# Neighbour sums of a graph layer: key one-hots made for four units in one 16-bit comparison

## What is computed

```python
agg = jax.ops.segment_sum(x[src], dst, num_segments=x.shape[0])
h = x + agg
```

## Time and profile before

| | us |
|---|---|
| median of 3 runs | 3819.62 |
| lowest and highest | 3816.06, 3821.36 |
| the profiled execution | 3812.78 |
| its span | 3811.0 |
| busy in the span: PE, DVE, POOL, ACT | 3136.0, 2677.0, 2500.8, 1944.4 |
| first and last start of the row one-hots (L1933) | 3367.4, 3688.0 |
| first and last start of the sums (L1945) | 3379.6, 3693.1 |

### The profile page before, as it was taken

How to read it: one execution, slowest core, us unless ns; L and a number is a source line. 1 busy time by engine, 2 the same in 40 slices (tenths; PEclk the granted TensorE clock), 3 DMA queues, 4 the chain that set the end, 5 groups by cost and what they waited for, 6 DMA issues and landing times. The chain is left out here.

```text
span 3811.0 us, 89063 instructions
## 1 busy us (share of the span) xinstructions
PE 3136.0 (82%) x31400; PEld 1856.8 (49%) x31400; DVE 2677.0 (70%) x6673; ACT 1944.4 (51%) x5497; POOL 2500.8 (66%) x1949
## 2 busy tenths in 40 slices
PE   0369999999999999994629799797997978559886
PEld 0235555555555555553515455453554535347663
DVE  3538888888888888886745466464664647489972
ACT  3346556666665666651306455454554544158761
POOL 4488787687687687406378888888888870557620
PEclk9989999999999999996759899898998988579997
DMA  3323333333333333214222233232332322211210
GB/s 62 59 51 75 79 82 82 76 88 83 75 84 80 75 90 82 70 53 100 57 46 63 58 74 75 61 75 60 70 75 61 75 60 44 40 32 38 44 41 22
DMA packets 417512, 249.11 MB, mean 65 GB/s; under 512 B 258173, under 2 KB 380449, under 8 KB 416562
## 3 DMA queue, kind: packets, MB, share of 16 engines
q0 software_dynamic: 97392, 70.80, 10.8%
q10 hardware_dynamic: 237600, 89.88, 9.3%
q1 hardware_dynamic: 82086, 82.74, 8.7%
HBM read 135.21 MB, written 105.95 MB: 63 GB/s over the span
## 5 line engine op out<-in xcount | busy, mean ns | idle before, releaser
L1011 PE MATMUL L_e_ps_z<-L_e_xT,L_w_abs 128*128 128x500 f32 x2700 | 1382.6, 622 | 193.1 <-ACT L_e_rl L1127 192.3
L598 POOL DMA_INDIRECT L_e_tiles<-in_x_dram,src_tile x800 | 1107.9, 1385 | 350.3 <-issue 234.1
L598 POOL DMA_INDIRECT L_e_tiles<-x_d,src_tile x800 | 1010.2, 1263 | 250.2 <-issue 237.7
L1127 ACT ACTIVATE L_e_rl<-L_e_ps_z 128x500 f32<-128x500 f32 x1350 | 778.8, 586 | 573.0 <-PE L_e_ps_z L1011 571.0
L1319 DVE SCALAR_TENSOR_TENSOR L_e_acc<-L_e_acc,L_e_row,L_e_ps_v 128x130 f32<-128x130 f32 (+1 forms) x1440 | 447.4, 311 | 620.2 <-PE L_e_ps_v L1073 434.4
L1011 PEld LDWEIGHTS L_e_ps_z<-L_e_xT,L_w_abs 128*128 128x128 f32 x2700 | 444.7, 191 | 480.1 <-issue 370.1
L642 ACT ACTIVATE L_e_xs<-L_e_tiles 125x64 f32 x1800 | 308.8, 248 | 390.1 <-issue 255.6
L1073 PEld LDWEIGHTS L_e_ps_v<-L_e_xs,L_e_p 125*64 125x64 f32 x8400 | 318.3, 141 | 357.8 <-issue 175.8
L1073 PE MATMUL L_e_ps_v<-L_e_xs,L_e_p 125*64 125x65 f32 x8400 | 425.8, 235 | 19.4 <-DVE L_e_acc L1319 15.5
L1118 ACT ACTIVATE L_e_xT<-L_e_ps_x 128x500 f32<-128x500 f32 x450 | 264.8, 588 | 236.5 <-PE L_e_ps_x L998 236.4
L1230 DVE SCALAR_TENSOR_TENSOR L_e_f<-L_e_rl,L_sign,L_e_f 128x500 f32<-128x500 f32 x450 | 329.1, 731 | 9.9 <-ACT L_e_rl L1127 6.6
(11 more groups left out here) (323 smaller groups left out, 4211.0 us busy)
## 6 DMA issues: line engine op xcount, KB each, us to landing
L_v_d<-L_e_acc ACTq DMA_DIRECT2D x225, 260.0 KB
L_e_dlb<-dloc_d SPq DMA_DIRECT2D x90, 468.8 KB, 5.1
L_v_d<-L_e_acc ACTq DMA_DIRECT2D x225, 130.0 KB
L_e_tiles<-in_x_dram,src_tile POOLq DMA_INDIRECT x800
L_e_tiles<-x_d,src_tile POOLq DMA_INDIRECT x800
L_e_lim<-limits_d SPq DMA_DIRECT2D x180, 39.1 KB
L_max_d<-L_e_me SPq DMA_DIRECT2D x45, 78.1 KB
L_e_lim<-limits_d SPq DMA_DIRECT2D x180, 19.5 KB
```

The costliest lines, as they stand in the source:

```text
L598: pool.indirect_dma_start(lay.tiles[:, g % TR * D:(g % TR + 1) * D], None, lay.x_rows, bass.IndirectOffsetOnAxis(k.src_tile[:, g:g + 1], 0 ...
L1011: pe.matmul(ps_z[part % ZR][:, 0:QT], lay.w_abs[:, part * 128:(part + 1) * 128], xT[q][:], start=True, stop=True).then_inc(s["z_ready"], 1)
L1127: act.activation(rl[n % NE][:], ps_z[part % ZR][:, 0:QT], ACT.Relu, scale=1.0 - SLOPE).then_inc(s["relu_done"], 1)
```

## The change

The key one-hots are made as the row one-hots are: one comparison for four units, units innermost, with both operands bf16 tensors. For this a table `keys4` holds each of the 200 keys four times, and `key16` holds `key_of` in bf16; both are made once, by two DVE instructions at the head of the block ahead of the turns. A ring of 3 buffers of four units takes the place of 10 buffers of one. A count matmul now reads its streamed operand with a step of four elements (8 bytes), where it read adjacent elements. The semaphore `hot` rises by four with each comparison.

```diff
-    HR, KR, CR, PQ = 3, 10, 3, 4
+    HR, KR, CR, PQ = 3, 3, 3, 4
...
+        keys4 = sbuf(nc, octx, nm + "keys4", [T, KEYS, HU], BF16)
+        key16 = sbuf(nc, octx, nm + "key16", [T, EU], BF16)
...
                 def _(dve):
+                    dve.tensor_copy(keys4[:], keys_n[:].unsqueeze(2).to_broadcast([T, KEYS, HU]))
+                    dve.tensor_copy(key16[:], key_of[:])
                     dve.wait_ge(s["part"], 1)
...
-            ohk = [sbuf(nc, ctx, f"{nm}ohk{r}", [T, KEYS], BF16) for r in range(KR)]
+            ohk = [sbuf(nc, ctx, f"{nm}ohk{r}", [T, KEYS, HU], BF16) for r in range(KR)]
...
-                            pe.matmul(ps_c[n % 2][0:RW, u * KEYS:(u + 1) * KEYS], ohr[v // HU % HR][:, :, v % HU], ohk[v % KR][:],
+                            pe.matmul(ps_c[n % 2][0:RW, u * KEYS:(u + 1) * KEYS], ohr[v // HU % HR][:, :, v % HU], ohk[v // HU % KR][:, :, v % HU],
                                       start=True, stop=True).then_inc(s["counted"], 1)
...
-                    def hot_keys(v):
-                        if v >= KR:
-                            dve.wait_ge(s["counted"], v - KR + 1)
-                        dve.tensor_scalar(ohk[v % KR][:], keys_n[:], key_of[:, v:v + 1], None, ALU.is_equal).then_inc(s["hot"], 1)
+                    def hot_keys(g):
+                        if g >= KR:
+                            dve.wait_ge(s["counted"], (g - KR + 1) * HU)
+                        dve.tensor_tensor(ohk[g % KR][:], keys4[:],
+                                          key16[:, g * HU:(g + 1) * HU].unsqueeze(1).to_broadcast([T, KEYS, HU]),
+                                          ALU.is_equal).then_inc(s["hot"], HU)
...
                             if u % HU == 0:
                                 hot_rows((i * GR_U + u) // HU)
-                            hot_keys(i * GR_U + u)
+                                hot_keys((i * GR_U + u) // HU)
```

## The result

| | before | changed |
|---|---|---|
| median of the runs, us | 3820.49 | 3874.05 |
| lowest and highest | 3816.06, 3822.50 | 3872.22, 3877.01 |
| the profiled execution | 3812.78 | 3873.93 |
| its span | 3811.0 | 3872.1 |
| stage, first row one-hot to the end of the last sum | 326.0 | 378.8 |

The change is slower: ratio 1.0145, 95% interval 1.0129 to 1.0161, 54 us by the medians. The forecast was 3793, range 3784 to 3811.

A forecast was written before the change was run, and what follows sets the result against it. DVE was taken as the bound. Turns 281, block waits 11, start 2 and ends 4 gave a 298 us stage against 326; -28 + 0.5 + 0.3 = -27 from the median 3819.6 gave 3793, range 3784 to 3811.

The forecast's parts named there:

- the unpriced piece: Count matmuls on PE reading 200 columns 8 bytes apart: addition between 0 and 85 ns a matmul, taken as 0.
- the strided stream at double rate: Rival on PE's 1024 count matmuls: 0.085 us more each, three quarters showing, 65 us; +38, so 3858; chance 0.10.
- The cost on DVE: Key comparison of 800 elements takes 0.49 us, not held up beside gathers; a DVE turn becomes 3.70 us.
- What is late next: PE and ACT set the pace: turns of 4.15 us, 4.70 with `add_block`; stage 298 us against 326.
- The added pieces: Two DVE instructions ahead of the turns, 0.5 us; PE's first wait for four units, 0.3; ring of 12 units, nothing.
- The rival of the f32 rate: DVE's key comparison takes 0.91 us, turns 5.38 us, DVE stays the bound: +19, so 3838; chance 0.02.

The follow-up runs named there:

- the adjacent stream: The changed kernel, but each count matmul streams 200 adjacent elements of the four-unit one-hot, so counts are of the wrong keys: 3799.49 us, ratio 0.9946.
- the pairs: The changed kernel with each unit's 200 keys adjacent, each key number stored twice in a row and no `keys4`: 3801.71 us, ratio 0.9951.
- the run with units outermost: The changed kernel with each unit's 200 keys adjacent, the comparison reading each key number 200 times in a row, no `keys4`: 3886.33 us, ratio 1.0157.

## Why the prediction was wrong, point by point

**The step that failed** is the unpriced piece: "I take 0". Between an addition of 0 and of 85 ns a count matmul, the value is the upper end, 0.085 us. The reason given for 0 was that the weight loads' 15 ns says nothing of the stream; true, but it left no row that says 0 either. Advanced Engine Details and Errata, section SBUF Cachelines, of the Trainium skill, by which two reads on each 16-byte line are at full speed, is contradicted for this stream: at 8 bytes two reads fall on a line, and a count matmul takes 0.17 us instead of 0.085.

**The rival that came true** is the strided stream at double rate, given 0.10. Its mechanism and place were right, its price was low: 1024 x 0.085 = 87 us, of which I let three quarters show, because PE has slack behind j = 0 and 1. But only one pair's slack is left there. In a turn without `add_block` seven of the eight steps from pair to pair grow by 0.17 to 0.19 us and one stays, 1.27 us in all; in the 19 turns with both `add_block` and `add_rows` all eight grow, 1.44 us. With each of 63 turns at the shortest of its kind, the sum is 276.7 us with the adjacent stream and 359.6 with the change, so 83 of the 87 us show.

Some of it is made up in the seven turns with the first use of a block. They lie 18.8 us above their pace with the adjacent stream, 12.7 with the pairs and 8.2 with the change, since the block's chain of store, landing and load has longer turns to pass in (PE's weight loads wait 12.8, 10.9 and 7.8 us for blocks). So from the stage of the adjacent run (309.1), which differs in the step alone, to that of the change (378.8) it is 70 us, and 75 from the paired form (303.4), where I had 65. The gain that this is set against is 17 and 23 us by the same stages, where I had 28. So +38 became +54.

**The cost on DVE** was right: 0.49 us from start to start forecast for the comparison, 0.48 measured (3375.91 to 3376.39 in the changed kernel), and its form is not held up beside gathers (its longest record is 616 ns). The reasoning by elements alone, under which two tensors lose to a tensor and a scalar, did not decide, as forecast: with the adjacent stream the same comparison gains.

**What is late next** was right too. With the stream adjacent the turns are 4.15 and 4.7 us, as read from the earlier trace rows, and the kernel gains 23 us (adjacent) and 21 us (pairs), against 27 forecast for it. The difference is in the stage, 309.1 and 303.4 us against 298, and most of it in the turns with a first use of a block, for which I took 11 us and which lie 18.8 and 12.7 above their pace. At three of them in the adjacent run and one with the pairs, behind waits of 1.6 to 3.3 us, PE's granted clock fell to half. Gathers were waited for too, three times and twice.

**The added pieces** were cheap: the two instructions ahead of the turns have records of 576 and 685 ns and end before ACT's copy is done, so they cost nothing, against 0.5 allowed. The ring of three groups costs nothing that the runs show: with it the turns are 4.15 us.

**The rival of the f32 rate** did not come with the change, but came in the run with units outermost, and was under-priced there by the gathers that it held up: 64 us over the kernel before, where the rival had 19.

**Small sums** of the forecast don't come out: 27 us are 0.70% and not 0.72, and its own range, from no waits for blocks to half the gain, would be 3782 to 3806 and not 3785 to 3802. Neither bears on the result.

## What to carry to other kernels

When a layout is changed so that one engine writes or compares faster, price the reads of every engine that takes it as a stream, above all on the engine that is late next. A comparison of two bf16 tensors needed only two adjacent elements innermost to be fast here, so the other axis can be chosen for the reader. An unpriced read with ends 0 and double on the coming bound belongs in the range with its full price, and an edit of two lines that lets it read a fixed table in that form prices it.

## What the runs showed of the hardware that was not expected

- The streamed operand of a bf16 matmul costs by the bytes spanned, or by something in proportion to them: 0.085 us for 200 adjacent columns, 0.09 at 4 bytes a column (in single steps or as two of four), 0.17 at 8 and 0.345 at 16. The weight load with a step of 8 bytes took 113 ns against 96 adjacent, and the shortest turns 4.15 us against 4.14.
- The record of a comparison of two bf16 tensors on DVE, 800 elements, was 570 ns with two or four adjacent elements innermost in every operand, and 987 with one operand standing still innermost. A copy of 800 bf16 elements with a source standing still innermost took 576.
- Beside the slower form POOL took up to 5.1 us for a gather piece, instead of 1.21.
